# A selective-scan block with scan tiles of 8 states x 16 channels, 32-column sums on TensorE, and the convolution formed by TensorE

## The reference

```python
xz = x @ W_in.T                         # 128 -> 512: x_ssm (256 channels) and z (256)
xc = conv1d(x_ssm, conv_w, causal, 4 taps, each channel by itself) + conv_b
x_ssm = silu(xc)
proj = x_ssm @ W_x.T                    # 16 B's, 16 C's and one number for dt
dt = softplus(proj[..., -1:] * W_dt[:, 0] + b_dt)        # one for each channel
A = -exp(A_log)                                          # 256 channels x 16 states
h = exp(dt * A) * h + (x_ssm * dt) * B                   # 256 x 16 recurrences over time
y = sum_over_16_states(h * C) + x_ssm * D_param
y = (y * silu(z)) @ W_out.T
x = layernorm(x + y)
h = silu(x @ w1 * s1) * (x @ w2 * s2); h = gelu(h @ h1 * s); h = gelu(h @ h2 * s)
x = layernorm(x + h @ w3 * s3)
```

## Time and profile before

| | us |
|---|---|
| median of three runs | 1126.44 |
| the profiled execution, whole | 1125.33 |
| its span, first to last instruction | 1123.5 |
| busy PE / DVE / ACT / POOL | 1028.0 / 1029.9 / 901.6 / 854.8 |

### The profile page before, as it was taken

The page is one execution under the profiler, slowest core; times in us unless marked ns, Lnnn a source line. Parts: engine busy times, 40 slices in busy tenths (PEclk is TensorE's granted clock), DMA queues, the critical chain, the costliest instruction groups (busy, mean ns, idle before and its releaser), DMA issues.

```text
span 1123.5 us, 14735 instructions
## 1 busy us (share of the span) xinstructions
PE 1028.0 (92%) x4928; PEld 649.0 (58%) x4928; DVE 1029.9 (92%) x1484; ACT 901.6 (80%) x1257; POOL 854.8 (76%) x499
## 2 busy tenths in 40 slices
PE   4656999999999999999999999999999999998997
PEld 1435566575756556565656657575665757555543
DVE  4999999999999999999999999999999999999511
ACT  7664988989798988979898898989889897987231
POOL 1677878878797888869788887978788797888540
PEclk8686999999999999999999999999999999999999
DMA  4762340705325070622507061340707043060000
GB/s 179 274 240 80 128 184 10 320 11 200 132 79 242 12 319 11 253 78 92 230 21 310 11 266 65 143 188 15 306 10 306 25 180 141 31 291 1 19 10 10
DMA packets 44060, 152.28 MB, mean 136 GB/s; under 512 B 4560, under 2 KB 24016, under 8 KB 27728
## 3 DMA queue, kind: packets, MB, share of 16 engines
q1 hardware_dynamic: 43600, 151.02, 34.1%
q10 hardware_dynamic: 384, 0.32, 0.1%
HBM read 146.08 MB, written 5.24 MB: 135 GB/s over the span
## 4 chain that ended last, share of the span: by engine, by line
PE 69%; ACT 16%; DVE 7%; issue 6%; POOL 2%; DMA 0%; ACTq 0%; DVEq 0%; POOLq 0%
PE G L705 33%; PE Y L690 14%; ACT dA L335 6%; PE G L727 4%; PE G L712 3%; ACT g L378 3%; DVE hb L598 3%; PE G L673 2%; PE Y L653 2%; PE Y L735 2%; PE G L657 2%; DVE U L591 2%; PE G L709 1%; ACT L351 1%; ACT xs L351 1%
## 5 line engine op out<-in xcount | busy, mean ns | idle before, releaser
L320 POOL TENSOR_TENSOR pb<-hb,cbc 128x1024 f32<-128x1024 f32 x256 | 602.9, 2363 | 179.9 <-DVE hb L598 139.6
L598 DVE TENSOR_TENSOR_SCAN hb<-dA,U 128x512 f32<-128x512 f32 x512 | 594.8, 1205 | 0.0
L335 ACT ACTIVATE dA<-dt,negA 128x510 f32<-128x510 f32 x512 | 342.2, 712 | 62.3 <-DVE hb L598 60.8
L591 DVE TENSOR_TENSOR U<-X,bbc 128x512 f32<-128x512 f32 x512 | 327.0, 686 | 7.2 <-ACT X L341 6.4
L690 PEld LDWEIGHTS Y<-ident,pb 128*128 128x128 f32 x2048 | 244.1, 145 | 111.0 <-issue 73.0
L690 PE MATMUL Y<-ident,pb 128*128 128x128 f32 x2048 | 272.1, 280 | 31.9 <-POOL pb L320 31.9
L705 PE MATMUL G<-hid,h_sb 128*128 128x512 f32 x512 | 232.6, 598 | 1.0 <-ACT g L494 0.8
L705 PE MATMUL G<-g,h_sb 128*128 128x512 f32 x512 | 229.8, 593 | 0.0
L705 PEld LDWEIGHTS G<-hid,h_sb 128*128 128x128 f32 x512 | 96.0, 193 | 110.5 <-issue 107.7
L705 PEld LDWEIGHTS G<-g,h_sb 128*128 128x128 f32 x512 | 92.6, 190 | 94.5 <-issue 90.3
L310 POOL TENSOR_TENSOR hid<-hid,g 128x512 f32<-128x512 f32 x64 | 80.1, 1273 | 7.8 <-ACT g L494 7.8
(11 more groups left out here) (91 smaller groups left out, 997.7 us busy)
## 6 DMA issues: line engine op xcount, KB each, us to landing
cbc<-scr SPq DMA_DIRECT2D x64, 1024.0 KB, 7.8
bbc<-scr SPq DMA_DIRECT2D x63, 1024.0 KB, 9.1
xT_sb<-xT_d SPq DMA_DIRECT2D x16, 256.0 KB, 2.7
xtok_sb<-xtok_d SPq DMA_DIRECT2D x16, 256.0 KB, 2.9
out_d<-r SPq DMA_DIRECT2D x16, 256.0 KB, 2.4
h_sb<-h_d SPq DMA_DIRECT2D x2, 1024.0 KB, 22.3
bbc<-scr SPq DMA_DIRECT2D x2, 512.0 KB, 4.6
scr<-rows SPq DMA_DIRECT2D x62, 16.0 KB, 1.5
```

The source lines that it names most:

```text
L320: nc.gpsimd.tensor_tensor(pb[:, qs:qs + 2, :], hb[:, hs:hs + 2, :], cbc[:, n:n + 2, :], ALU.mult).then_inc(s_p, 1)
L335: nc.scalar.activation(halves(dA[:, u % DA_RING, :])[:, :, 1:SEQ], halves(dt[:, par, c, :])[:, :, 1:SEQ], ACT.Exp, scale=negA[:, c, n:n + ...
L591: nc.vector.tensor_tensor(U[i][:], X[:], bbc[:, n + i, :], ALU.mult).then_inc(s_u, 1)
L598: nc.vector.tensor_tensor_scan(hb[:, 2 * (v % H_PAIRS) + i, :], dA[:, u % DA_RING, :], U[i][:], 0.0, ALU.mult, ALU.add).then_inc(s_h, 1)
```

## The change

**Tiles.** A scan tile is now 8 states x 16 channels: partition s*16+d. A block still has 32 tiles of 512 columns. Now B and C are the same for all tiles of a half of the states (`brep`, `crep`: 2 x 256 KB each), and what differs from tile to tile is dt and dt*x, which must be copied to 8 groups of partitions: `dtr` and `xdr`, 1 MB for each of four loads, through memory. `X` holds B and is filled three times a round. Groups of four tiles (`GT`) share a sum step, and three slots hold the loads.

**Sums.** `sum_group` multiplies a tile by a 0/1 matrix of 128 x 32 into 32 partitions of `Y`; four tiles go to the four quarters. `start_sum` multiplies x by diag(D). The result has channels on partitions, so `turn`, `copy_turned` and `times_D` go, and z is projected the other way round.

**Convolution.** `wc` holds W_in times each tap; four matmuls from shifted columns add up in PSUM; ACT copies with the bias; DVE's `taps` go.

```diff
-TILES = NS * NC
+SN, SD = 8, 16
+NG = NS // SN
+GT = 4
+GROUPS = NG * DI // SD // GT
+TILES = GROUPS * GT
+SLOTS = 3
...
+            def store_steps(b, c, scr, x, s_stored):
+                to = scr[b % 2, c].rearrange("e d q t -> q (e d) t")
+                sp.dma_start(to, x[:, c, :]).then_inc(s_stored[c], 16)
+            def spread_steps(b, c, e, scr, o, s_o):
+                slot = group_no(b, c, e) % SLOTS
+                piece = scr[b % 2, c, e].rearrange("d q t -> d (q t)")
+                sp.dma_start(flat(o[:, slot, :, :]), piece.unsqueeze(0).to_broadcast([SN, SD, GT * TB])).then_inc(s_o[slot], 16)
...
+                if front:
+                    sp.wait_ge(s_rows, A + 1)
+                    store_rows(A, range(NT))
+                    sp.wait_ge(s_dt, 2 * A + 1)
+                    store_steps(A, 0, scr_dt, dts, s_dts)
+                    sp.wait_ge(s_xd, 2 * A + 1)
+                    store_steps(A, 0, scr_xd, xds, s_xds)
+                    sp.wait_ge(s_dts[0], 16 * (A + 1))
+                    sp.wait_ge(s_dA, TILES * j + 4 * GT)
+                    spread_steps(A, 0, 0, scr_dt, dtr, s_dtr)
...
-                if v >= P_PAIRS or not first:
-                    pool.wait_ge(s_y, STEPS * j + v - P_PAIRS + 1)
+                if v >= P_PAIRS or b > 0:
+                    pool.wait_ge(s_y, GROUPS * b + (v - P_PAIRS) // 2 + 1)
...
-                    if v == 11 and front:
-                        add_dt(A, 1 - par)
-                    if v == 13 and front:
-                        times_dt(A, 1 - par, 0)
+                    if v == 9 and front:
+                        add_dt(A, 0)
+                        times_dt(A, 0)
+                    if v == 11 and front:
+                        add_dt(A, 1)
+                    if v == 12 and front:
+                        times_dt(A, 1)
...
+            def fill_X(b, i):
+                g = i % 2
+                if i < 2:
+                    act.wait_ge(s_b[g], 16 * (b + 1))
+                if b > 0 or i > 0:
+                    act.wait_ge(s_u, TILES * b + (0, 2 * GT, 6 * GT)[i])
+                nc.scalar.activation(X[:], brep[:, g, :], ACT.Copy).then_inc(s_X, 1)
...
-            def taps(b, c):
-                for s in range(1, TAPS):
...
+            def in_conv(b, c):
+                to = bank_in(b, c)
+                for s in range(TAPS):
+                    last = nc.tensor.matmul(halves(to)[:, :, s:SEQ], wc[:, TAPS - 1 - s, c * P:(c + 1) * P],
+                                            halves(xT_sb[:])[:, :, 0:SEQ - s], start=(s == 0), stop=(s == TAPS - 1),
+                                            skip_group_check=True)
+                last.then_inc(s_ip, 1)
...
-            def sum_pair(b, v):
...
+            def sum_group(b, k):
+                c, e, _ = load_of(k)
+                pe.wait_ge(s_p, STEPS * b + 2 * k + 2)
+                for q in range(GT):
+                    rows32 = slice(q * 2 * SD, (q + 1) * 2 * SD)
+                    last = nc.tensor.matmul(Y[c][rows32, :], sel_sb[:, e, :], pb[:, (GT * k + q) % (2 * P_PAIRS), :],
+                                            start=False, stop=(k % (GROUPS // NC) == GROUPS // NC - 1),
+                                            skip_group_check=True, tile_position=(0, q * 2 * SD))
                 last.then_inc(s_y, 1)
```

More of the change, by code:

```diff
@@ L443, in _ @@
             softplus_part(1, ACT.Abs)
+            softplus_part(1, ACT.Relu)
+            softplus_rest(1)
+            act.wait_ge(s_alog, 16)
+            nc.scalar.activation(negA[:], negA[:], ACT.Exp).then_inc(s_aexp, 1)
+            act.wait_ge(s_aexp, 1)
+            nc.scalar.mul(negA[:], negA[:], -1.0).then_inc(s_aneg, 1)
+            copy_z(0, 0)
+            copy_z(0, 1)
+            fill_X(0, 0)
             act.wait_ge(s_aneg, 1)
             act.wait_ge(s_zero, 3)
[L446 removed]
@@ L447, in _, with run @@
-            decay(0, 0, 1, True)
-            softplus_part(1, ACT.Relu)
-            decay(0, 0, 2, True)
-            decay(0, 0, 3, True)
-            times_D(0, 0, 0)
-            softplus_rest(1)
-            for u in range(4, AHEAD):
-                decay(0, 0, u, True)
-            def run(j, par, scan, intake, front, back, tail):
-                first = isinstance(j, int) and j == 0
+            for u in range(AHEAD):
+                decay(0, u)
+            def run(j, scan, intake, front, back, tail):
@@ L674, in dt_proj @@
                 last.then_inc(s_dtb, 1)
-            def start_sum(b, par, c):
-                if not (isinstance(b, int) and b == 0):
-                    pe.wait_ge(s_gy, 2 * b - 1 + c)
-                pe.wait_ge(s_xD, 2 * b + c + 1)
-                for t in range(NT):
-                    last = nc.tensor.matmul(Y[c][:, t, :], tile_of(xD[:], t), ident[:], is_transpose=True,
-                                            start=(t == 0), stop=False, skip_group_check=True)
-                last.then_inc(s_start, 1)
@@ L695, in turn, with start_sum @@
-            def turn(b, c):
-                pe.wait_ge(s_gy, 2 * b + 1 + c)
-                for t in range(NT):
-                    last = nc.tensor.transpose(tile_of(BTURN[c], t), gy[:, t, c * P:(c + 1) * P], ident[:])
-                last.then_inc(s_gt, 1)
+            def start_sum(b, c):
+                if b > 0:
+                    pe.wait_ge(s_gate, 2 * b - 1 + c)
+                pe.wait_ge(s_xs, 2 * b + 1 + c)
+                nc.tensor.matmul(Y[c][:], diagD[:, c, :], xs[:, b % 2, c, :], start=True, stop=False,
+                                 skip_group_check=True).then_inc(s_start, 1)
```

689 lines of the change are left out of this document (337 added, 352 removed).

## The result

The changed kernel takes 1495.93 us (median of 4 runs, 1492.18 to 1501.76) where the kernel before took 1125.88 beside it: a ratio of 1.329, 95% interval 1.324 to 1.334. The forecast was 1109 with a range to 1140.

A forecast was written before the change was run, and what follows sets the result against it. DVE bounds the kernel before (64.6 us a round), PE the changed one (63.5). Start +15.4, rounds and tail -8.8, -4.4, -13.2, -2.7, -1.5, -2.0: -17.2, median 1109; own range 1097 to 1124, overall 1083 to 1140.

The forecast's parts named there:

- Data late: Rival: memory write and read-back cost 5 us more, B lands 2 us late each round; +24, 1133; chance 0.09.
- margin of 3 us for B: B's copy lands near 21.5 us after DVE's v = 9 starts; DVE's next block starts at 24.5.
- The start: Work before the first tile: first tile moves from 20.65 to near 36 us, +15.4.
- PE's terms: PE's round: sum group 1.09 us, convolution +5.16 in all; busy 62.2, with waits 63.5.
- The wait at the gate: DVE at the second half's gate (v = 1) waits some 3 us a round for the last group's sum.
- Round 0: First round: twelve DVE taps go, -8.8 us.
- PE is not the bound: Rival: the round falls to DVE's 59.8 to 61; another -30 to -44, 1065 to 1079; chance 0.13.
- the chain: POOL, store, copy, then ACT's decay of the next block: dt's copy lands at 14.3 us, just when ACT asks.
- ACT as the bound: Rival: ACT's waits remain, from x1's turn to softplus; round 65.1 or 66.4, +19 to +35, 1128 to 1144; chance 0.27.

The follow-up runs named there:

- the kernel before showed afterwards with 8: The kernel before, with its 1 MB copies of B and C written as 8 times 16 partitions (outermost dimension 8) instead of 128: 1490.62 us.
- the shapes repaired in two steps: Changed kernel with copies of outermost dimension 16 instead of 8: 1228.46 us; then also each store in four pieces of 32 partitions: 1136.50 us.
- rows of 128: Against the 1136.5 us kernel (copies of 16, split stores), each copy takes one row of memory to all 128 partitions; output not the reference's: 1121.03 us.
- one tap: Against the 1121.03 us kernel, one shifted matmul for each convolution half instead of four; output not the reference's: 1119.92 us.
- 1.6 us less of it, off the chain: Against the 1121.03 us kernel with all taps, the gelu between the H products writes 64 of 512 columns from the second block on: 1121.37 us.

## Why the prediction was wrong

The step that failed is this one: "1 MB takes 2.5 us at the 420 GB/s of the burst, so 10 MB are 25 us of 63: bandwidth is no bound." The rate was read from copies whose outermost dimension is the 128 partitions, and put on copies with 8 and stores with 4, though the change's own lines show these shapes. None of the rows that it read shows a transfer of such a shape, so the rate had no source for them. With the 117 GB/s that the kernel before showed afterwards with 8, the sum would have been 8 x 1.049 MB / 0.117 = 72 us for the copies of dt and dt*x alone, above every engine. Measured: 85 us a round at 133 GB/s.

Step by step, after that:

- *Data late* was the right rival with a wrong size. It took 5 us for the way through memory and 24 in all; it was about 21 us a round and 370 in all. Its margin of 3 us for B turned into ACT waiting 161.7 us in 15 rounds.
- *The start.* Forecast first tile 36; 51.6 in the changed kernel, 42.3 and 38.6 with the shapes repaired in two steps, 36.1 with rows of 128.
- *PE's terms* held for the two new kinds: 0.99 for a group and 0.10 behind it against 1.09, 3.50 for a convolution half against 3.44. PE's busy time was still 63.2 against 62.2, with shorter waits in part making up for it. PE sets a round of 63.84 in place of 63.5 once the copies are as fast as assumed. The wait at the gate (3.3 us) and the busy times of DVE, ACT and POOL came out to 0.2 us.
- *Round 0* was mis-sized: -8.8 us for the taps, but it took 61.7 against 64.25 before, not 55.5. DVE's busy time there is 55.4, as forecast; it waits 6.3 us for X, and PE's clock is granted at 0.78. With one tap the same round is 57.5, though the clock is at 0.68 there: the taps on PE are on the path. That (6.2 us), 1.0 in round 1, 12 x 0.4 in rounds 2 to 13 and 1.2 in round 14 are the 13 us between the 1108.1 forecast for the profiled execution and its 1121.47.
- *"PE is not the bound"* priced a lighter PE at 30 to 44 us. With 5.2 us less on PE it is worth 1 us, for two reasons: at full clock something stands at 63.3, most likely the chain over softplus, store and copy, and in eight of twelve rounds the clock falls for 3.4 us. The forecast had the chain (dt's copy lands "just when ACT asks") but gave it no length of its own, and it reckoned PE's clock as full whatever PE had to do.
- *ACT as the bound* is refuted as to ACT's load: with PE busy 63.1 of 63.9 us, 1.6 us less of it, off the chain, left the rounds alone (63.87 us against 63.84).
